# Layer 1: the gather's index copy on GpSimd moved one block ahead

## What is computed

```python
h = relu(layernorm(x))
# layer 0: an edge MLP, summed over the edges of a node
e = softplus(concat(h[src], h[dst]) @ W0 + b0)
e = softplus(e @ W1 + b1) @ W2 + b2
x = x + segment_sum(e, src)
# layer 1: sum of the neighbours, node MLP, batch norm, residual
h = relu(layernorm(x))
z = h + segment_sum(h[src], dst)
z = relu(z @ W1 + b1) @ W2 + b2
z = relu((z - mean(z)) * rsqrt(var(z) + eps) * gamma + beta)
x = x + (h + z)
```

## Time and profile before

| | us |
|---|---|
| median of 3 runs | 2134.45 |
| lowest and highest | 2132.37, 2137.1 |
| the profiled execution, its own time | 2146.18 |
| its span in the trace | 2144.5 |
| mean granted TensorE clock, as a share of full speed | 0.899 |

### The profile page before, as it was taken

How to read it: one execution, slowest core, us unless ns; L and a number is a source line. 1 busy time by engine, 2 the same in 40 slices (tenths; PEclk the granted TensorE clock), 3 DMA queues, 4 the chain that set the end, 5 groups by cost and what they waited for, 6 DMA issues and landing times. The chain is left out here.

```text
span 2144.5 us, 37416 instructions
## 1 busy us (share of the span) xinstructions
PE 1499.0 (70%) x10067; PEld 1102.8 (51%) x10067; DVE 1074.0 (50%) x3261; ACT 976.5 (46%) x2310; POOL 1084.1 (51%) x1151
## 2 busy tenths in 40 slices
PE   0011129999999999999999999547656566666655
PEld 0011117777777777777777777423444334444434
DVE  5899963444444444544444445414533333333344
ACT  0366656666666666666666666301211111111144
POOL 0699964343434343344343434266666666666700
PEclk9999999999999999999999999768977777777765
DMA  1344432433333343343434343322322222222259
GB/s 30 88 122 123 125 109 60 107 90 97 94 93 99 88 103 84 80 106 88 99 85 102 88 98 94 68 40 53 65 51 51 51 52 51 52 51 51 35 170 312
DMA packets 341017, 187.87 MB, mean 88 GB/s; under 512 B 281564, under 2 KB 307561, under 8 KB 340967
## 3 DMA queue, kind: packets, MB, share of 16 engines
q1 hardware_dynamic: 292388, 129.09, 23.1%
q0 software_dynamic: 28224, 32.57, 9.0%
q10 hardware_dynamic: 20354, 25.65, 3.3%
HBM read 131.42 MB, written 55.79 MB: 87 GB/s over the span
## 5 line engine op out<-in xcount | busy, mean ns | idle before, releaser
L784 POOL DMA_INDIRECT fast_gathered<-h_table,fast_gather_i x441 | 421.3, 955 | 625.9 <-PE bank L928 409.5
L1118 POOL DMA_INDIRECT fast_gathered<-h_neighbours_table,fast_index_i x441 | 425.4, 965 | 198.8 <-issue 187.4
L1020 ACT ACTIVATE fast_h<-bank,b_s 128x384 f32<-128x384 f32 (+1 forms) x490 | 301.0, 622 | 329.6 <-PE bank L939 196.1
L1179 PE MATMUL node_sums<-twice,fast_self_rows 128*64 128x128 f32 x784 | 136.2, 401 | 249.2 <-DMA fast_gathered<-h_neighbours_table,fast_index_i 231.3
L1027 ACT ACTIVATE fast_h<-fast_h 128x384 f32<-128x384 f32 (+1 forms) x490 | 273.8, 559 | 0.0
L1210 ACT ACTIVATE fast_z_in<-node_sums 128x512 f32<-128x512 f32 x49 | 29.3, 597 | 532.4 <-PE node_sums L1185 359.3
L816 DVE TENSOR_TENSOR fast_message<-bank,b_s 128x192 f32<-128x192 f32 x147 | 52.6, 358 | 437.4 <-PE bank L974 347.8
L1179 PEld LDWEIGHTS node_sums<-twice,fast_self_rows 128*64 128x64 f32 x784 | 114.4, 209 | 292.1 <-issue 249.6
L1185 PE MATMUL node_sums<-fast_hot,fast_gathered 128*64 128x256 f32 (+1 forms) x980 | 221.2, 442 | 24.5 <-issue 24.2
L953 PE MATMUL bank<-fast_h,w_s 128*128 128x384 f32 (+1 forms) x490 | 222.4, 536 | 0.5 <-ACT fast_h L1027 0.5
L1164 DVE BATCH_NORM_STATS2 z_stats<-z_t (+1 forms) x48 | 33.3, 694 | 361.2 <-issue 182.1
(11 more groups left out here) (231 smaller groups left out, 2677.4 us busy)
## 6 DMA issues: line engine op xcount, KB each, us to landing
fast_local<-local_rows SPq DMA_DIRECT2D x49, 576.0 KB
h_neighbours_table<-fast_h_rows SPq DMA_DIRECT2D x49, 320.0 KB
fast_self_rows<-h_neighbours_table SPq DMA_DIRECT2D x49, 320.0 KB
h_table<-prep_normed ACTq DMA_DIRECT2D x49, 256.0 KB, 2.3
fast_own_rows<-h_table SPq DMA_DIRECT2D x49, 256.0 KB
x_plus_h<-fast_x SPq DMA_DIRECT2D x49, 256.0 KB
finish_resid<-x_plus_h SPq DMA_DIRECT2D x49, 256.0 KB
prep_xin<-in_x SPq DMA_DIRECT2D x48, 256.0 KB
```

The costliest lines, as they stand in the source:

```text
L784: pool.indirect_dma_start(gathered[slot][:, j * D:(j + 1) * D], None, h0_t, bass.IndirectOffsetOnAxis(ap=gather_i[q][:, n:n + 1], axis=0))\
L1020: A(to[at][:, 0:w], psum[:, 0:w], ACT.Exp, bias=b_s[:, :]).then_inc(done, 1)
L1118: pool.indirect_dma_start(gathered[q][:, c * MW:(c + 1) * MW], None, h1_t, bass.IndirectOffsetOnAxis(ap=index_i[q][:, c:c + 1], axis=0))\
L1179: nc.tensor.matmul(banks[6 + q % 2][h * D:(h + 1) * D, k * P:(k + 1) * P], self_rows[q][:, at:at + D], twice[:, :], start=(k == 0), stop=F ...
```

## The change

GpSimd's body is split in two kinds, `copy(n)` and `gather(n)` for n = 0, 1, 2, and `rounds` gets the list copy(0), gather(0), copy(1), gather(1), copy(2), gather(2), with lag 0 for copies and lag 1 for gathers. At step u GpSimd thus copies the indices of block u and gathers those of block u - 1. The ring wait on `gather_done` stays with copy(0); the waits on `nodes_summed` and `matched` go to gather(0). The wait on `index_ready` stays in front of each stretch of gathers, with the same value as before for the block.

```diff
@@ -1106,20 +1106,30 @@
 
                     @block.gpsimd
                     def _(pool):
-                        def gather(b, q, turn):
-                            wait_from(pool, gather_done[q], 16 * CT * turn, passed_pool)
-                            wait_from(pool, nodes_summed, b - RING + 1, passed_pool)
-                            wait_from(pool, matched, b - RING + 1, passed_pool)
-                            for n in range(CT // COPIED):
+                        def copy(n):
+                            def body(b, q, turn):
+                                if n == 0:
+                                    wait_from(pool, gather_done[q], 16 * CT * turn, passed_pool)
                                 nc.gpsimd.tensor_copy(index_i[q][:, n * COPIED:(n + 1) * COPIED],
                                                       far_src[:, bass.ds(b * CT + n * COPIED, COPIED)]).then_inc(index_ready, 1)
+                            return body
+
+                        def gather(n):
+                            def body(b, q, turn):
+                                if n == 0:
+                                    wait_from(pool, nodes_summed, b - RING + 1, passed_pool)
+                                    wait_from(pool, matched, b - RING + 1, passed_pool)
                                 hold(pool, index_ready, CT // COPIED * b + n + 1, passed_pool)
                                 for c in range(n * COPIED, (n + 1) * COPIED):
                                     pool.indirect_dma_start(
                                         gathered[q][:, c * MW:(c + 1) * MW], None, h1_t,
                                         bass.IndirectOffsetOnAxis(ap=index_i[q][:, c:c + 1], axis=0))\
                                         .then_inc(gather_done[q], 16)
-                        rounds(pool, [(0, gather)], BLOCKS)
+                            return body
+                        stages = []
+                        for n in range(CT // COPIED):
+                            stages += [(0, copy(n)), (1, gather(n))]
+                        rounds(pool, stages, BLOCKS)
 
                     @block.vector
                     def _(dve):
```

## The result

The changed kernel takes 2141.91 us (median of 9 runs, 2139.65 to 2148.71) against 2134.45 us (9 runs beside them, 2130.52 to 2140.66): ratio 1.0039, 95% interval 1.0024 to 1.0054, 7.5 us slower. The forecast was 2069.3 us, range 2050 to 2086. Its profiled execution took 2145.63 us, with a span of 2143.0.

What follows compares the result with a forecast made beforehand. GpSimd's instruction stream was taken to bound layer 1. Gains of 64.8 us (copy wait) and 0.3 us (start) sum to 65.1 us, bringing the profiled 2146.18 to 2081.1 and the median 2134.45 to 2069.3 us; range 2050 to 2086.

Steps and rivals of the forecast that it cites:

- The bound: Layer 1's loop: GpSimd's instruction stream, gather after gather, sets the pace at 13.65 us a block.
- The wait for the copy: Gap from copy to gather in layer 1's loop falls from 1.00 to 0.46 us, 120 times: 64.8 us gained.
- rival (a): The gap behind a loop copy falls below 0.27 us: up to 26 us more gain, 2043 us; chance 0.17.
- (c): Any gather behind a register-form GpSimd copy idles 0.8 us, with or without the wait: 2134 us; chance 0.03.
- (d): GpSimd's queue cannot pass an unfinished copy, so column 0 has three waits in the open gap: 2178 us; chance 0.05.
- The ring waits: Waits on nodes_summed and matched, moved behind copy 0 of a block, are satisfied long before: cost nothing.
- The start: Layer 1's first blocks: earlier gain is absorbed at block 7, the ring doesn't hold blocks 9 and 10; 0.3 us gained.
- The end: After block 48's last gather: PE is as late there, all after shifts as a whole; nothing counted.
- (b): Gain partly kept back by column 0, the ring at blocks 9 and 10, or DVE: 2075 to 2100 us; chance 0.13.
- PE busy without a wait for DMA: Sign in the loop that the forecast is wrong, with PE as the bound; no size given.

Runs made afterwards that it cites:

- e4: The kernel before, with each copy of three index columns put ahead of the last gather of the stretch before it; ratio 0.9599, 2012.7 us.
- e18: The changed kernel with PE multiplying only the first and last of nine gathered columns of a block in layer 1; ratio 0.9955 to the kernel before.
- e16: The changed kernel with a memset of an unused 128x512 tile behind every copy, where the kernel before takes about 2097 us; ratio 0.9960 to it.
- e7: The changed kernel with a memset of an unused 128x512 tile behind every copy, where the kernel before takes about 2138 us; ratio 0.9940 to it.

## Why the prediction was wrong, step by step

- **The bound** was read rightly: GpSimd's instruction stream paced layer 1 of the kernel before.
- **The wait for the copy**: right in kind, small in size. 0.54 us a copy was taken, 0.65 measured (0.81 to 0.16), 78 us in place of 64.8: half of rival (a)'s extra. The argument for stopping at 0.27 us, that the 0.30 us between plain gathers belongs to the gather, did not hold: behind a copy it is 0.16. Where nothing else is slow (e4), the same gap gave 84 us. That the gather gets queued while others run was right too, so rivals (c) and (d) did not happen.
- **The ring waits**: this is the step that failed. It said they cost nothing, and that if the cover went, "the engine next in line is PE with 8.46 us a block" against 12.03, so that "3.6 us are left". It is the term that was put at nothing, and it cost about as much as the wait had: some 63 us saved at the copies from 1540 to 1980 us, and as much spent at the ring. Both numbers took PE's pace from a trace in which GpSimd pauses 0.81 us every third gather. The runs show that on kind B PE's, DVE's and SyncE's pace depends on how closely GpSimd's gathers follow each other: 11 matmuls in 17 us. Even with PE's work cut (e18) the block took 13.39 us. The room was no property of PE.
- **The start**: "PE, ACT and DVE begin layer 1 slowly" was taken as given. That was the warning. Their matmuls at the start stood 1.4, 2.1 and 2.8 us apart with "issue" ahead of them (rows below), where GpSimd's stretch was 3.94 us, the very value the change was to bring to the loop. Had I asked what made the start slow, the mechanism would have been a rival.
- **The end**: counted at nothing; 7.7 us more in the first pair of traces, 12.2 in the second. It turns "no gain" into "slower" in the first comparison.
- **Rivals**: (b) named the ring, but for two blocks, not for the whole loop; none named a mechanism that slows the other engines. "PE busy without a wait for DMA" did not come either: PE is idle, waiting for its own instructions.

The warning in PE's timeline of the kernel before:

```profile
1407.26 0.42 PE L1185 MATMUL node_sums<-fast_hot,fast_gathered 128*64 128x256 f32 x1 [1.02 <-issue]
1408.67 0.38 PE L1185 MATMUL node_sums<-fast_hot,fast_gathered 128*64 128x256 f32 x1 [1.00 <-issue]
...
1419.23 0.37 PE L1185 MATMUL node_sums<-fast_hot,fast_gathered 128*64 128x128 f32 x1 [1.73 <-issue]
1422.03 0.59 PE L1185 MATMUL node_sums<-fast_hot,fast_gathered 128*64 128x256 f32 x1 [2.42 <-issue]
```

## What to carry to other kernels

A slack of the next engine in line holds only if that engine's pace does not depend on what is being sped up; look in the same trace for a stretch where the sped-up pattern already runs, and at the others' "issue" time there. Starts of unrelated engines at multiples of one odd interval (0.70 us here) point to a shared cause, not to their work. After removing a pause from a row of gathers on GpSimd, measure on more than one chip (0.9599 and 1.0024 for one program here), and try a pause behind every third gather before giving up the change (a memset of 0.52 us here, which kept 0.6% and 0.4%).

## What was not expected of the hardware

- Gathers issued by GpSimd at three in 4.1 us or closer (4.2 with pauses after each) bring the queues of PE, DVE and SyncE to about one instruction in 0.70 us on kind B, for microseconds on end; at three in 4.32 or 4.47 us single steps of 0.70 us are left in SyncE's queue, and PE has no slow stretches in the steady part. In the first trace it ended 2.7 us after the last gather. A fifth of the bytes in as many packets changes nothing, nor does the depth of GpSimd's queue.
- Chips differ in this: on kind A there are no such stretches at three gathers in 3.83 us (0.9599 against 1.0024 for one program), and the kernel before is 2% faster there. Layer 0, which also gathers, is 25 to 42 us shorter there too. The same moves in SyncE's queue take 29 ns each on kind A and 3 to 712 ns on kind B (e16 and e7). What differs between the chips, whether it is the chip or something else that runs beside it, and by which path an issued gather slows other engines' queues, no run here shows; one chip of kind B was met twice and was of that kind both times.
